# Fillers, one subtraction and the first heads' order in a fused convolution and expert kernel

## The reference, cut to what matters

```
K   = 2 * Re( sum_n Cs[h,n] * exp(dtA[h,n] * l) )          # l = 0..1023
u_m = x * mask
y   = (causal convolution of u_m with K, + u_m * D) * mask
logits = y @ route_w.T ; top 1 of 8 -> gate
out = x + sum_e gate_e * (y @ A_e.T) @ Bw_e.T
```

## Time and profile before

| | us |
|---|---|
| median of 3 runs | 586.90 (586.86 to 586.94) |
| the profiled execution | 586.32 |
| its span | 584.5 |
| PE busy | 569.4 (97%) |
| POOL, DVE, ACT busy | 426.5, 486.8, 380.2 |

### The profile page before, as it was taken

One profiled execution on the slowest core, in us unless ns is written; L12 is line 12 of the kernel. 1 busy time (PEld: TensorE's weight loads), 2 busy tenths in 40 slices (PEclk: granted clock), 3 DMA queues, 4 the chain that ended last, 5 costly groups with the idle time before them and its releaser, 6 DMA issues.

```text
span 584.5 us, 13307 instructions
## 1 busy us (share of the span) xinstructions
PE 569.4 (97%) x3524; PEld 515.7 (88%) x3524; DVE 486.8 (83%) x1348; ACT 380.2 (65%) x1185; POOL 426.5 (73%) x569
## 2 busy tenths in 40 slices
PE   4899999999999999999999999999999999999996
PEld 3788998999999899899899899999989989989995
DVE  7988788888888888888888888888888888888875
ACT  4787667666676666767666676666666666666630
POOL 5797868777677867868786786877768777776540
PEclk9899999999999999999999999999999999999999
DMA  7133543543453454454354355345345345435422
GB/s 146 57 88 129 163 128 126 154 140 117 152 163 96 150 163 105 144 161 123 125 161 139 112 157 163 96 149 163 99 147 162 104 147 159 126 126 156 143 77 97
DMA packets 38187, 77.67 MB, mean 133 GB/s; under 512 B 12824, under 2 KB 21466, under 8 KB 38114
## 3 DMA queue, kind: packets, MB, share of 16 engines
q1 hardware_dynamic: 28514, 43.30, 29.0%
q10 hardware_dynamic: 9600, 33.53, 14.4%
HBM read 43.16 MB, written 33.65 MB: 131 GB/s over the span
## 4 chain that ended last, share of the span: by engine, by line
PE 95%; DVE 1%; ACT 1%; issue 1%; POOL 0%; ACTq 0%; DVEq 0%
PE psYo L1196 21%; PE psZ L1222 20%; PE psYe L1196 13%; PE psS L1196 11%; PE psO L1297 5%; PE psO L1299 5%; PE psO L1302 5%; PE psXe L1210 5%; PE psXo L1210 5%; PE psO L1253 2%; PE psZ L1286 1%; PE psO L1248 0%; PE psYe L1345 0%; DVE psS L1033 0%; DVE ost L1072 0%
## 5 line engine op out<-in xcount | busy, mean ns | idle before, releaser
L1033 DVE SCALAR_TENSOR_TENSOR psS<-Sf,tab,psS 64x128 f32<-64x128 f32 x256 | 91.9, 359 | 59.5 <-ACT Sf L733 53.1
L565 POOL TENSOR_TENSOR Slo<-Sf,Shi 128x384 fp32r<-128x384 f32 x64 | 65.2, 1019 | 92.8 <-ACT Shi L738 92.7
L1222 PE MATMUL psZ<-Wt,Y 128*128 128x136 f32 x1024 | 129.2, 279 | 0.0
L1222 PEld LDWEIGHTS psZ<-Wt,Y 128*128 128x128 f32 x1024 | 123.3, 190 | 0.1
L1072 DVE TENSOR_TENSOR ost<-psO,xt 128x512 f32<-128x512 f32 x127 | 87.1, 690 | 0.8 <-PE psO L1302 0.7
L558 POOL TENSOR_TENSOR Xlo<-xeven,Xhi 128x512 fp32r<-128x512 f32 x63 | 81.7, 1296 | 0.0
L537 POOL TENSOR_TENSOR Wg<-same,cross 128x256 f32<-128x256 f32 x59 | 43.6, 739 | 39.5 <-ACT cross L671 25.5
L517 POOL TENSOR_TENSOR both<-coarse,fine 128x512 f32<-128x512 f32 x64 | 67.9, 1061 | 1.3 <-ACT fine L647 1.2
L733 ACT ACTIVATE Sf<-psS 128x128 f32<-128x128 f32 x64 | 17.8, 278 | 77.3 <-PE psS L1196 77.2
L738 ACT ACTIVATE Shi<-Sf 128x384 fp32r<-128x384 f32 x64 | 33.7, 526 | 51.8 <-DVE Sf L1037 51.8
L671 ACT ACTIVATE cross<-Grev,tabm 64x256 f32<-64x256 f32 x118 | 59.7, 506 | 2.6
(11 more groups left out here) (217 smaller groups left out, 1575.5 us busy)
## 6 DMA issues: line engine op xcount, KB each, us to landing
xt<-in_x_dram SPq DMA_DIRECT2D x64, 512.0 KB, 4.9
out_dram<-ost ACTq DMA_DIRECT2D x62, 512.0 KB, 5.1
Traw<-kdram SPq DMA_DIRECT2D x64, 128.0 KB, 2.9
kdram<-krow SPq DMA_DIRECT2D x59, 1.5 KB
A_nat<-in_L_ffn_A_dram ACTq DMA_DIRECT2D x1, 512.0 KB, 4.1
B_nat<-in_L_ffn_Bw_dram SPq DMA_DIRECT2D x8, 64.0 KB, 2.9
out_dram<-ost SPq DMA_DIRECT2D x2, 256.0 KB, 2.1
out_dram<-ost ACTq DMA_DIRECT2D x1, 256.0 KB, 2.0
```

The costliest lines, as they stand in the source:

```text
L565: pool.tensor_tensor(Slo[h.s2][:, :], Sf[h.s2][:, :], Shi[h.s2][:, :].bitcast(F32), ALU.subtract).then_inc(slo_done, 1)
L1033: dve.scalar_tensor_tensor(psS[to, new], Sf[h.s2][fr, old], tab2[fr, BR, h.n:h.n + 1], psS[to, new], ALU.mult, ALU.add).then_inc(brought_d ...
L1222: last = pe.matmul(psZ[:, 0:NW], Y[:, j, c, :], Wt[:, 2 * c + j, :], start=(j == 0 and c == 0), stop=(j == 1 and c == NE - 1), skip_group_ ...
```

## The change

The number of fillers is changed in two places of PE's list, and three pairs of calls change places: on DVE the low part of x of head 1 (odd blocks) and the first carry, on ACT the first `t_hi` and the second `g_hi`, and on ACT `first_state` and `t_hi` of head 1.

```diff
@@ ACT
             s_hi(first[0])
+            t_hi(first[0])
             g_hi(first[1])
-            t_hi(first[0])
             b_hi(first[2])
@@ ACT
             act.activation(warm[:, :], quarter[:, :], ACT.Exp)
+            first_state(first[1])
             t_hi(first[1])
-            first_state(first[1])
             run_steps(step)
@@ DVE
+            carry(first[0])
             x_lo(first[1])
-            carry(first[0])
             turn_k(first[1])
@@ PE
-            keep_busy(psO[0], 2)
+            keep_busy(psO[0], 4)
             pe.wait_ge(br_set, 1)
             pe.wait_ge(pack2_done, 3)
             pe.wait_ge(w_done, 1)
@@ PE
             pe.wait_ge(blo_set, 2)
-            keep_busy(psY[0], 6)
+            keep_busy(psY[0], 2)
             inputs(first[2])
```

## The result

The changed kernel takes 588.88 us in the median of 14 executions (588.21 to 590.66), the kernel before beside it 587.08 (586.20 to 587.56): ratio 1.0038, 95% interval 1.0027 to 1.0048. It is slower, by 1.8 us in the medians. The forecast was 588.9.

The account below looks back on a forecast made before the run. PE bounds the kernel, gapless from 37.42, so a shift there shifts the end. Inputs of head 2 late 1.86 plus ACT's swap 0.16 give +2.0: 588.3, with the median's 0.6 588.9; range 587.0 to 590.5.

Parts of the forecast that it names:

- The main step: On PE ahead of the odd turn of head 2: a 2.6 us standstill for DVE's x_lo of head 1, to 26.05.
- The fillers ahead of the packing: PE, gap of 0.89 us: four more records, 0.5 to 0.85 us, cost 0, keep the clock up after 20.1; Sf 1.0 sooner.
- The first low stretch: PE's clock at 1.2 GHz from 20.1 to 23.5 in the kernel before; forecast to go, chance 0.65.
- a rival's term (1.0): PE doesn't wait decisively for x_lo: about 1.0 us sooner at head 1, 585.9; chance 0.10.
- The second fall: PE's clock falls around 27, after the eight transposes (0.75); inputs of head 2 end at 29.5, 1.86 us late.
- this case and its 0.7: The clock falls within PE's wait for x_lo, so the eight transposes run at the low pace too: 0.7 us more.
- some 1.6: PE's own queue at bring of head 1: some 1.6 us late, under the 2.0 of POOL's path.
- rival 1: The clock holds through PE's wait for x_lo: 0.90 + 0.16 = +1.06, 588.0 us; chance 0.20.
- The clamp: DVE, at 29.05: took 0.64 where the median is 0.23; a credit of 0 to 0.4 us, taken as 0.
- ACT's swap: first_state and t_hi of head 1 change places: Thi one slot later, costing 0.16 us through POOL; earlier carry worth 0.
- The rule of the Trainium skill on gaps: PE's clock falls only after a long enough gap between matmuls; by its figure the 2.6 us standstill leaves it up.

Follow-up runs that it names:

- x_lo alone: Kernel before with only x_lo of head 1 put behind the first carry on DVE: 590.94 us, ratio 1.0071.
- six fillers behind the wait: Changed kernel with six fillers in place of two ahead of the third inputs, behind PE's wait for x_lo: 590.59 us, ratio 1.0067.
- fillers in the wait: Changed kernel with ten more fillers in PE's wait for x_lo, behind the inputs of head 1: 588.28 us, ratio 1.0026.
- timeline of four fillers: Kernel before with four fillers ahead of the packing and ACT's first_state ahead of t_hi of head 1: 585.84 us, ratio 0.9991.

## Why the prediction was right, and where its sizes were off

*The number owes something to luck.* It was 588.3 for an execution like the profiled one, plus the 0.6 by which the median of the kernel before lay above its profiled execution. The profiled execution of the changed kernel took 589.48, 1.2 more than 588.3: the shift at head 1 was 3.22 and not 2.0. The medians lie only 1.8 apart; eight of the 14 executions have a higher mean clock than the profiled one.

*The main step held.* PE's wait for x_lo was put at 2.6 us with the turn at 26.05; it was 2.65 and 26.17. Undoing it alone takes the loss away, doing it alone makes it twice as large.

*The fillers ahead of the packing held in this trace, not in all.* The first low stretch went, at no cost, and Sf came at 22.81 (forecast 22.8). In three of ten traces with four fillers it did not go. The step took the fillers' pace as given, 0.5 to 0.85 us for the four records added; it left out that at the upper pace the two fillers that were there end sooner as well, and the wait is 1.6 to 2.0 us in place of 0.4 or less. The worth of this without the wait, which I had only as a rival's term (1.0), is 1.0 in the profiled spans (584.5 to 583.5).

*The second fall came, at another time.* The step "I expect a second fall, around 27, when the eight transposes are through" is mis-sized. It was at 25.3, within the wait, and the clock came back at 32.1: 6.8 us low. The eight transposes ran at the low pace as well (26.17 to 28.04, 1.87 for 1.06), the fillers took 1.01 for 0.85; the tables 0.51 for 0.50 and the inputs 1.07 for 1.06 were as priced. So the inputs of head 2 ended 2.97 late and not 1.86. The prediction named this case and its 0.7, but did not take it as the likely one. Nor did it let the clock stay low for more than 3.4 us: the states' product of head 0 ran at the low pace as well, and `bring` of head 1 started 2.99 late (34.34), where some 1.6 was forecast. In the traces of x_lo alone and of six fillers behind the wait the second fall came as forecast, behind the transposes (28.9 and 29.1, 3.4 us each).

*The clock has no fixed timetable.* Here the forecast was weakest. I read the times of the falls from one execution and took them for all. In the profiles PE's pace rose at 12.0 in one kernel and behind 16 in another with the same instructions up to there, and the changed kernel's 14 executions hold several outcomes. In three the mean clock is 0.999 to 1.0, which leaves no room for a low stretch of 3.4 us: it held through the wait (my rival 1, 588.0; they take 588.24 to 588.47). In five it is 0.997, as one fall of 3.4 us gives; whether that is the fall forecast behind the wait or the old one near 20 no trace shows, and they take as little (588.21 to 588.68, one 589.07). In six it was low for 6.8 us or more (589.48 to 590.66), which neither the forecast nor rival 1 had. That the median is 588.88 comes of how these halves happen to balance.

*The clamp was priced at 0 with bounds of 0 to 0.4 less; it has both signs.* The reason given, that POOL is as busy a little later, was wrong: POOL stood still from 31.2 on, for 5.04 us. In the changed kernel's profile the clamp took 0.23 and low_fraction 0.34, a credit of 0.42; with fillers in the wait the two cost 0.67 more than before. The bound above was missing.

*ACT's swap: 0.16 forecast, 0.20 measured in the timeline of four fillers,* and POOL, not the carry, set the place, as said. In the changed kernel itself ACT's queue wasn't the last there: Sf of head 1 waited 0.39 for PE's bring, and Thi, which needs no bring, stood behind it. So there the swap cost about 0.6, an estimate from these rows. This is the sum: 2.97 late at the inputs, less the clamp's 0.42, plus that 0.39, plus 0.2, gives 3.1 of the 3.22.

*The rule of the Trainium skill on gaps* (TensorE: Matmul & The Clock Gate, HAM oscillation) was the ground of rival 1: a gap as long as this one would leave the clock up. The trace doesn't agree: the clock fell within a gap of 2.65 us. The run with the fillers in the wait shows that the gap does matter (none of its executions above 589.4, six of 14 without them), and three of 14 executions of the changed kernel, at 0.999 to 1.0, kept the clock all the same. So as a yes or no the rule is not borne out: whether a gap of this size costs the clock differs between executions of one program.

*Left open:* why executions with a mean clock of 1.0 of the kernel before also take 587 to 588. Its profile counts the pace at 15.6 as 1.00 though it is low, so a low start is perhaps not counted; no run tested that.

## What to carry to other kernels

Before a call is moved behind a longer one, look for who waits on what it frees, not only on what it makes: x_lo's result was wanted by the bring of head 1 at 31, but the bank it reads was wanted at 24. Fillers are worth their place only in a gap; the same records cost nothing ahead of a wait, hold the clock in one, and stand on the path behind one. A filler is a number of records and not a time: eight filled the gap ahead of the packing at the low pace (1.91 us) and left 1.8 us of it open at the upper one (1.06 us). Where the clock can fall, look at the times execution by execution: a median between two groups describes none of its executions.

## What the runs showed of the hardware that was not expected

One set of instructions has its clock changes at different times from execution to execution. Up to the packing the kernel before and the one with only x_lo moved are the same on PE; two fillers ran at 0.21 us a record at 15.60 in the first, and in the second four records took 0.61 from 14.71 on, 0.11 to 0.12 each. The first then fell at 20.1 and was back at 23.5, the second fell at 18.7 and was back at 22.1. The faster start bought nothing there: the packing waits for ACT and began at 17.55 and 17.48, so PE only stood still for longer, 2.16 us in place of 0.89.

A DVE operation of 128x128 (the clamp) took 0.23 us where POOL stood still and 0.64, 0.65, 0.85 or 0.97 where POOL was at work beside it; the same work moved by 1 us thus costs up to 0.7 more or 0.4 less.
